# Attention and expert layer on one core: parts of queries and keys stored once, the repeats moved into the loads

## The chip, the cores and the metric

The kernel runs on one core of a Trainium2 chip. The metric is the device time of one execution in microseconds (us). Before the change three executions took 955.06, 957.02 and 960.02 us; the median is 957.02 us.

## The reference

The input is x with 8 batches of 512 tokens of 128 numbers, all in 32-bit floats. For each batch an attention block and then an expert block are computed:

```python
q = split_heads(einsum('bsd,kd->bsk', x, q_proj_weight))      # 16 heads of 8 numbers
k, v = the same with k_proj_weight, v_proj_weight
scores = einsum('bhtc,bhkc->bhtk', q, k) * 8 ** -0.5          # causal: -inf above the diagonal
out = einsum('bhtk,bhkc->bhtc', softmax(scores), v)           # heads side by side, then o_proj_weight
x = layernorm(x + out @ o_proj_weight.T)
# experts: 64 experts of width 64, sigmoid router, 4 of 8 groups, 8 experts kept, weights scaled by 2.5
h = silu(x @ Wg[e]) * (x @ Wu[e]) * coef[:, e]                # for every expert e; coef is 0 where not chosen
x = layernorm(x + sum_e h @ Wd[e] + silu(x @ SWg) * (x @ SWu) @ SWd)
```

All 64 experts are computed for all tokens, and the coefficient is zero where an expert is not chosen.

## The kernel before

**Parts.** A score is a product of 8 numbers for each head, and it is needed nearly in 32-bit precision, while the matmuls run on bf16. So each query and each key is split into three bf16 parts, whose sum is the number. The nine products of a part of q with a part of k are all taken in one matmul: its contraction has 3 x 3 x 8 = 72 rows. The stack of queries holds, in row (a, b, c), part a of the number c of the query; the stack of keys holds in that row part b. Each part thus stands three times in its stack.

**Way of the parts.** `q` and `k` (L776) project a batch; ScalarE writes part 0 (L900), VectorE the rest and parts 1 and 2 (L1148, L1154, L1157) into `qk_parts`, 128 rows (c, head) by 512 tokens. `store_part` stores one part to DRAM, in one DMA that writes it three times (L645): `q_rows_dram` and `k_rows_dram` have the dimensions [2 batches, a, b, c, head, token], part p of q goes to [a = p, all b], part p of k to [all a, b = p]. There are six stores a batch, counted by `parts_stored`. Then the task `rs` loads the rows of two heads, 72 rows of 2 x 512 bf16 numbers (2 KB a row), into both stacks (L700), two DMAs. Eight `rs` tasks a batch fill the stacks; these are rings of four places for a pair of heads (`RING_PAIRS` = 4), and `stacked[j]` counts the landings of place j, 16 for each DMA.

**Users of the stacks.** The task `mx` computes the scores of a head in three steps (L790), from which VectorE takes the largest of each row (L1182). When four heads are done, `mn` and `mT` turn the negated maxima into two further rows of the stack of queries (`max_rows`, L1207, loaded by L707), and the task `st` computes the transposed scores less the maximum from 96 rows (L808). ScalarE takes the exponential (L914), `pv` multiplies with v (L820). The `rs` for the place of an older pair waits until the last `st` of that pair is done.

**Experts.** For each of 32 pairs of experts and one shared unit TensorE computes gate (`g`) and up (`u`), three matmuls each (L749 to L751), and the down product (`d`, L864 to L866 or L879). GpSimd multiplies with the coefficients (L993), which a DMA has spread over the 128 rows (`coef_b`, L726, one for two units, 512 KB of writes each), and computes the low part for `d` (L997).

**Order.** There is no runtime planner. The tables FIRST, SECOND, THIRD, STEADY and EXPERTS give each task a place on a line, `order()` sorts them, and each engine goes through that one list and does its share of each task, in that order, with waits on semaphores. The attention of batch n + 1 is interleaved with the experts of batch n. Every DMA is issued by the sync engine's queue (SP), which is therefore in order too: a task whose wait is not over holds up everything behind it. Until the first expert TensorE does filler matmuls that nobody reads (L745, `FILL`; 62 after the first v).

Of the kernel before, what the change touches and what calls it, by code (L numbers as in the profile page):

```python
# [8 lines left out]
BF16 = mybir.dt.bfloat16  # L9
# [4 lines left out]
P = 128  # L14
B, S, D = 8, 512, 128
NH, C = 16, 8
# [15 lines left out]
STACK_PAIRS = NH // 2  # L32
RING_PAIRS = RING // 2
SPLIT_BY_DVE = 3
CHUNKS = 9
PARTS = 3
MAX_PARTS = 2
QK_ROWS = PARTS * PARTS * C
# [393 lines left out]
def build(nc, x, xT, wqT, wkT, wvT, woT, rwT, bias, Wg, Wu, Wd, SWgu, SWd, ident, causal, out):  # L432
    x_tok = x.rearrange("(b t p) d -> b p t d", t=NT, p=P)
    out_tok = out.rearrange("(b t p) d -> b p t d", t=NT, p=P)

    q_rows_dram = nc.dram_tensor("q_rows_dram", [2, PARTS, PARTS, C, NH, S], BF16).ap()
    k_rows_dram = nc.dram_tensor("k_rows_dram", [2, PARTS, PARTS, C, NH, S], BF16).ap()

    coef_dram = nc.dram_tensor("coef_dram", [2, E, S], F32).ap()

# [4 lines left out]
    with ExitStack() as ctx:  # L445
# [29 lines left out]
        qk_parts = sb("qk_parts", [P, 2, PARTS, S], BF16)  # L475
        rest = sb("rest", [P, S])
        q_stack = sb("q_stack", [STACK, RING, S], BF16)
        k_stack = sb("k_stack", [STACK, RING, S], BF16)
# [53 lines left out]
        stacked = [sem(f"stacked{j}") for j in range(RING_PAIRS)]  # L532
# [99 lines left out]
        def ring_nth(seg, n, j):  # L632

            return sum(t[0] == "rs" and t[2] % RING_PAIRS == j % RING_PAIRS and (t[1], t[2]) <= (n, j)
                       for t in seg.tasks)


        @block.sync
        def _(sp):
            sp.dma_start(wq_sb[:, :], wqT).then_inc(wq_in, 16)  # L640

            def store_part(kind, par, p):

                dst = q_rows_dram[par, p] if kind == "q" else k_rows_dram[par, :, p]
                sp.dma_start(dst.rearrange("o c h t -> (c h) o t"),  # L645
                             qk_parts[:, kind == "k", p, :].unsqueeze(1).to_broadcast([P, PARTS, S]))\
                    .then_inc(parts_stored, 16)

            def tasks(seg):
                for kind, n, i in seg.tasks:  # L650
                    task = (kind, n, i)
                    par = n % 2
                    if kind == "wld":
                        place = chunks[i][4]
                        if i - 2 >= SPLIT_BY_DVE:

                            sp.wait_ge(lo_done, i - 2 - SPLIT_BY_DVE + 1)
                        sp.dma_start(chunks[i][3], chunks[i][0]).then_inc(split_in[place], 16)
                    if kind == "ld":

                        after(sp, seg, sm_full, BANK_SM, ("v", n - 1, 0))
                        sp.dma_start(xT_sb[:, :], xT[n]).then_inc(x_in, 16)
                        if n == 0:
                            sp.dma_start(wk_sb[:, :], wkT).then_inc(wkv_in, 16)
                            sp.dma_start(wv_sb[:, :], wvT).then_inc(wkv_in, 16)
                    if kind == "ldtok":

                        before = seg.last(("x1",), task)
                        if before:
                            after(sp, seg, ob_free, BANK_O, ("oproj", before[1], 0))  # L670
                        after(sp, seg, out_ready, ("finx",), seg.last(("finx",), task))
                        sp.dma_start(y[:, :, :], x_tok[n]).then_inc(xtok_in, 16)
                    if kind == "q" and n == 0:
                        sp.dma_start(id_sb[:, :], ident).then_inc(id_in, 16)
                        sp.dma_start(hid[:, 1, :], causal).then_inc(id_in, 16)
                    if kind == "rs" and (n, i) == (0, 1):
                        for dst, src in small:
                            sp.dma_start(dst[:, :], src).then_inc(w_in, 16)
                    if kind in ("q", "k"):

                        for j in range(STACK_PAIRS - RING_PAIRS, STACK_PAIRS):
                            if seg.nth(("rs",), ("rs", n - 2, j)):
                                sp.wait_ge(stacked[j % RING_PAIRS], 16 * 2 * ring_nth(seg, n - 2, j))
                        after(sp, seg, part1_done, ("q", "k"), task)
                        store_part(kind, par, 0)
                    if kind in ("qsplit", "ksplit") and i == 1:
                        after(sp, seg, parts_done, ("q", "k"), (kind[0], n, 0))
                        for p in range(1, PARTS):
                            store_part(kind[0], par, p)
                    if kind == "rs" and (n, i) == (0, 0):  # L690
                        sp.wait_ge(zero_done, 2)
                        sp.wait_ge(const_done, 1)
                    if kind == "rs":

                        after(sp, seg, parts_stored, ("q", "k"), ("k", n, 0), 16 * PARTS)
                        before = (n, i - RING_PAIRS) if i >= RING_PAIRS else (n - 1, i + STACK_PAIRS - RING_PAIRS)
                        after(sp, seg, st_full, ("st",), ("st", before[0], 3 * 2 * (before[1] + 1) - 1))
                        hs, j = slice(2 * i, 2 * i + 2), i % RING_PAIRS
                        for stack, dram in ((q_stack, q_rows_dram), (k_stack, k_rows_dram)):
                            sp.dma_start(stack[0:QK_ROWS, 2 * j:2 * j + 2, :],  # L700
                                         dram[par, :, :, :, hs].rearrange("a b c h t -> (a b c) h t"))\
                                .then_inc(stacked[j], 16)
                    if kind == "mT":

                        after(sp, seg, sm_free, BANK_SM, (kind, n, i))
                        dst = q_stack[QK_ROWS:QK_ROWS + MAX_PARTS, HG * i % RING:HG * i % RING + HG, :]
                        sp.dma_start(dst.rearrange("p h (t q) -> p (h t) q", q=P), max_rows[:, :])\  # L707
                            .then_inc(maxrows_in[i], 16)
                    if kind == "attT" and n == B - 1:
                        after(sp, seg, ob_full, BANK_O, ("pv", n, GROUPS - 1))  # L710
                        sp.dma_start(wd_again, Wd[:, 0:PAIRS // 2 * D]).then_inc(wd_in, 16)
                    if kind == "coefT":
                        after(sp, seg, ob_free, BANK_O, task)
                        for t in range(2):
                            sp.dma_start(coef_dram[par].rearrange("e (k t q) -> t e k q", t=2, q=P)[t],
                                         coef_T[t * E:(t + 1) * E, :].rearrange("e (k q) -> e k q", q=P))\
                                .then_inc(coef_stored, 16)
                    if kind == "c":
                        after(sp, seg, coef_stored, ("coefT",), ("coefT", n, 0), 16 * 2)

                        before = ("h", n, 2 * i - 2) if i >= 2 else ("h", n - 1, UNITS - 3 + 2 * i)
                        after(sp, seg, h_done, ("h",), before)


                        src = coef_dram[par, 4 * i:4 * i + 4].rearrange("(e j) t -> e (j t)", e=2)
                        sp.dma_start(coef_b[:, i % 2, :, :].rearrange("p j t -> p (j t)"),  # L726
                                     src.unsqueeze(0).to_broadcast([I, 2, 2 * S])).then_inc(c_in[i % 2], 16)
                    if kind == "finx" and i == NT - 1:
                        after(sp, seg, out_ready, ("finx",), (kind, n, i))
                        sp.dma_start(out_tok[n], out_sb[:, :, :]).then_inc(out_stored, 16)  # L730

            tasks(ALL)
            sp.wait_ge(out_stored, 16 * B)


        @block.tensor
        def _(pe):
# [15 lines left out]
            def tasks(seg):  # L753
                before = None
                for kind, n, i in seg.tasks:
# [26 lines left out]
                    if kind == "mx":  # L782

                        h, part = divmod(i, 3)
                        if i % (3 * 2) == 0 and seg.nth(("rs",), ("rs", n, h // 2)):
                            pe.wait_ge(stacked[h // 2 % RING_PAIRS], 16 * 2 * ring_nth(seg, n, h // 2))
                        col = 0
                        for qb in MX_PARTS[part]:
                            wide = (qb + 1) * P
                            mm = pe.matmul(sm[:, col:col + wide], q_stack[0:QK_ROWS, h % RING, qb * P:(qb + 1) * P],  # L790
                                           k_stack[0:QK_ROWS, h % RING, 0:wide], start=True, stop=True)
                            col += wide
                        mm.then_inc(sm_full, 1)
# [511 lines left out]
```

## Time and profile before

| | |
|---|---|
| median of three executions | 957.02 us |
| span of the profiled execution (first to last instruction) | 952.6 us |
| mean granted clock of TensorE | 0.992 of 2.4 GHz |
| busy: TensorE, VectorE, GpSimd, ScalarE | 98%, 79%, 63%, 49% |
| moved by DMA | 121.70 MB |
| read from and written to HBM | 98.37 MB and 22.02 MB |

The profile is of one execution. PE is TensorE's matmuls and PEld its weight loads, DVE is VectorE, ACT ScalarE, POOL GpSimd, SPq the queue of the sync engine. The time of that execution differs from its span by what lies before the first and after the last instruction. A busy PE includes the fillers, and starts of matmuls overlap the end of the one before. From 340 us on one batch looks like the next (109 us each); the head (to about 125 us) and the end (from about 830 us) don't.

### The profile page before, as it was taken

How to read it: one execution, taken by the hardware profiler on the slowest of the kernel's cores; microseconds unless marked ns; L12 is line 12 of the kernel's file. 1: busy time of each engine (PE TensorE's matmuls, PEld its weight loads, DVE VectorE, ACT ScalarE, POOL GpSimd, SP SyncE). 2: the span in 40 equal slices, each digit the busy share in tenths (PEclk: the TensorE clock that was granted, in tenths of full speed). 3: DMA queues.
4: the chain of work that ended last, by engine and by line, in shares of the span. 5: the costliest groups of instructions: out<-in, count | busy, mean ns of one | idle time of the engine just before them, and what ended most of it. 6: DMA issues, size and time to landing. Idle time of an engine off the chain costs nothing.

```text
span 952.6 us, 16050 instructions
## 1 busy us (share of the span) xinstructions
PE 932.2 (98%) x5008; PEld 581.8 (61%) x5008; DVE 750.5 (79%) x2374; ACT 462.6 (49%) x866; POOL 598.4 (63%) x651
## 2 busy tenths in 40 slices
PE   8899999999999999999999999999999999999996
PEld 3355566666666666666666666675666666666664
DVE  5776887799877997799967997699967996578664
ACT  3355455455555545555555545555545555533221
POOL 2342247775777657775767757776667767775653
PEclk9799999999999999999999999999999999999998
DMA  8552154334534253433534254242633323242431
GB/s 292 159 167 67 50 176 146 113 104 136 181 96 135 92 184 126 136 114 96 192 115 136 84 179 138 94 136 73 211 117 113 114 88 95 87 162 82 138 129 56
DMA packets 64340, 121.70 MB, mean 128 GB/s; under 512 B 6656, under 2 KB 36224, under 8 KB 63744
## 3 DMA queue, kind: packets, MB, share of 16 engines
q1 hardware_dynamic: 64256, 120.67, 39.6%
q8 instruction: 41, 0.67, 0.3%
q14 instruction: 43, 0.35, 0.1%
HBM read 98.37 MB, written 22.02 MB: 126 GB/s over the span
## 4 chain that ended last, share of the span: by engine, by line
PE 85%; DVE 9%; issue 2%; DMA 2%; ACT 1%; SPq 0%; POOL 0%; POOLq 0%; DVEq 0%; ACTq 0%
PE acc L879 12%; PE ob L820 7%; PE sm L790 7%; PE st L808 7%; PE pu L749 6%; PE pg L749 5%; PE pg L751 5%; PE pg L750 5%; PE pu L750 5%; PE pu L751 5%; PE acc L745 4%; PE acc L864 2%; PE acc L866 2%; PE acc L865 2%; PE ob L832 2%
## 5 line engine op out<-in xcount | busy, mean ns | idle before, releaser
L993 POOL TENSOR_TENSOR hid<-hid,coef_b 128x512 f32<-128x512 f32 x240 | 309.5, 1290 | 134.7 <-DVE hid L1250 106.0
L1182 DVE CUSTOM_DVE_ANT_0 max_out<-sm,causal_sb 128x128 bf16<-128x128 f32 (+3 forms) x512 | 236.1, 486 | 60.6 <-PE sm L790 58.6
L942 ACT ACTIVATE hid<-pg 128x512 f32<-128x512 f32 x243 | 145.3, 598 | 245.2 <-PE pg L751 236.6
L914 ACT ACTIVATE probs<-st 128x512 f32<-128x512 f32 (+1 forms) x384 | 192.5, 525 | 75.8 <-PE st L808 74.1
L1241 DVE SCALAR_TENSOR_TENSOR hid<-hid,pg 128x512 f32<-128x512 f32 x243 | 165.8, 682 | 51.1 <-ACT hid L942 50.8
L997 POOL TENSOR_TENSOR hid_lo<-hid,hid_hi 128x512 fp32r<-128x512 f32 x112 | 144.0, 1285 | 75.7 <-ACT hid_hi L949 75.3
L1250 DVE TENSOR_TENSOR hid<-hid,pu 128x512 f32<-128x512 f32 x235 | 160.3, 682 | 30.0 <-PE pu L751 27.8
L979 POOL TENSOR_SCALAR_AFFINE_SELECT probs<-probs 128x256 f32<-128x256 f32 x256 | 97.8, 408 | 75.3 <-ACT probs L914 75.3
L790 PE MATMUL sm<-k_stack,q_stack 72*128 72x128 bf16 (+3 forms) x512 | 132.8, 307 | 3.7 <-DMA k_stack<-k_rows_dram 1.9
L749 PE MATMUL pg<-x_hi,wg_hi 128*128 128x512 f32 x240 | 127.7, 532 | 0.3 <-DVE hid L1241 0.2
L808 PE MATMUL st<-q_stack,k_stack 96*128 96x512 bf16 (+3 forms) x512 | 125.9, 304 | 0.2
L879 PE MATMUL acc<-hid,wd_sb 128*128 128x512 f32 x246 | 125.9, 593 | 0.0
L749 PE MATMUL pu<-x_hi,wu_hi 128*128 128x512 f32 x240 | 122.7, 511 | 0.9 <-DVE hid L1250 0.9
L751 PE MATMUL pg<-x_hi,wg_lo 128*128 128x512 f32 x240 | 94.8, 395 | 0.0
L750 PE MATMUL pu<-x_lo,wu_hi 128*128 128x512 f32 x240 | 94.8, 395 | 0.0
L751 PE MATMUL pu<-x_hi,wu_lo 128*128 128x512 f32 x240 | 94.7, 395 | 0.0
L750 PE MATMUL pg<-x_lo,wg_hi 128*128 128x512 f32 x240 | 94.6, 394 | 0.0
L808 PEld LDWEIGHTS st<-q_stack,k_stack 96*128 96x128 bf16 x512 | 45.1, 98 | 71.6 <-issue 52.9
L949 ACT ACTIVATE hid_hi<-hid 128x512 fp32r<-128x512 f32 x112 | 70.6, 630 | 36.5 <-POOL hid L993 31.6
L790 PEld LDWEIGHTS sm<-k_stack,q_stack 72*128 72x128 bf16 x512 | 43.7, 99 | 64.7 <-issue 41.4
L745 PE MATMUL acc<-filler 128*128 128x512 bf16 x240 | 81.0, 400 | 1.5 <-DVE filler L1019 1.5
L820 PE MATMUL ob<-probs,v_sb 128*32 128x512 f32 (+3 forms) x1024 | 75.6, 436 | 0.0
(161 smaller groups left out, 1295.4 us busy)
## 6 DMA issues: line engine op xcount, KB each, us to landing
coef_b<-coef_dram SPq DMA_DIRECT2D x128, 512.0 KB, 3.9
q_rows_dram<-qk_parts SPq DMA_DIRECT2D x24, 384.0 KB, 4.1
k_rows_dram<-qk_parts SPq DMA_DIRECT2D x24, 384.0 KB, 3.5
q_stack<-q_rows_dram SPq DMA_DIRECT2D x64, 144.0 KB
k_stack<-k_rows_dram SPq DMA_DIRECT2D x64, 144.0 KB
xT_sb<-in_xT SPq DMA_DIRECT2D x8, 256.0 KB, 3.8
y<-in_x SPq DMA_DIRECT2D x8, 256.0 KB, 3.9
out<-out_sb SPq DMA_DIRECT2D x8, 256.0 KB, 2.6
```

The costliest lines, as they stand in the source:

```text
L749: pe.matmul(psum[:, :], hi, x1_hi[:, par, :], start=True, stop=False)
L750: pe.matmul(psum[:, :], hi, x1_lo[:, par, :], start=False, stop=False)
L751: return pe.matmul(psum[:, :], lo, x1_hi[:, par, :], start=False, stop=True)
L790: mm = pe.matmul(sm[:, col:col + wide], q_stack[0:QK_ROWS, h % RING, qb * P:(qb + 1) * P], k_stack[0:QK_ROWS, h % RING, 0:wide], start=Tru ...
L808: mm = pe.matmul(st_bank[i % 2][:, col:col + wide], k_stack[:, h % RING, kb * P:(kb + 1) * P], q_stack[:, h % RING, kb * P:S], start=True, ...
L879: pe.matmul(acc[:, :], w, hid_of(n, i), start=first, stop=last).then_inc(d_full, 1)
L914: act.activation(probs[:, h % HG, at:at + wide], st_bank[i % 2][:, 0:wide], ACT.Exp, scale=C ** -0.5).then_inc(exp_done, 1)
L942: act.activation(hid_of(n, i), gate_bank(n, i)[:, :], ACT.Tanh, scale=0.5).then_inc(tanh_done, 1)
L993: pool.tensor_tensor(hid_of(n, i), hid_of(n, i), coef_b[:, half % 2, j, :], ALU.mult)\
L1182: last = dve.tensor_tensor_reduce(out=max_out[:, seg.nth(BANK_SM, task) % 2, col:col + wide], in0=sm_of(seg, task)[:, col:col + wide], in1 ...
L1241: dve.scalar_tensor_tensor(hid_of(n, i), hid_of(n, i), 1.0, gate_bank(n, i)[:, :], ALU.add, ALU.mult).then_inc(a_done, 1)
L1250: ins = dve.tensor_tensor(hid_of(n, i), hid_of(n, i), up_bank(n, i)[:, :], ALU.mult)
```

## The change

`store_part` writes each part once, and the DRAM tensors lose a dimension. The loads into the stacks read each row three times: the one load of the stack of keys does it with a repeat of step zero in front of its source pattern, and the load of the stack of queries becomes three, one for each part a, each with such a repeat over b. The counts of `stacked` become 4 DMAs for a pair of heads. Everything else, the order too, is as before.

```diff
+STACK_LOADS = 4
-    q_rows_dram = nc.dram_tensor("q_rows_dram", [2, PARTS, PARTS, C, NH, S], BF16).ap()
-    k_rows_dram = nc.dram_tensor("k_rows_dram", [2, PARTS, PARTS, C, NH, S], BF16).ap()
+    q_rows_dram = nc.dram_tensor("q_rows_dram", [2, PARTS, C, NH, S], BF16).ap()
+    k_rows_dram = nc.dram_tensor("k_rows_dram", [2, PARTS, C, NH, S], BF16).ap()
...
-                dst = q_rows_dram[par, p] if kind == "q" else k_rows_dram[par, :, p]
-                sp.dma_start(dst.rearrange("o c h t -> (c h) o t"),
-                             qk_parts[:, kind == "k", p, :].unsqueeze(1).to_broadcast([P, PARTS, S]))\
+                dst = q_rows_dram[par, p] if kind == "q" else k_rows_dram[par, p]
+                sp.dma_start(dst.rearrange("c h t -> (c h) t"), qk_parts[:, kind == "k", p, :])\
                     .then_inc(parts_stored, 16)
...
-                                sp.wait_ge(stacked[j % RING_PAIRS], 16 * 2 * ring_nth(seg, n - 2, j))
+                                sp.wait_ge(stacked[j % RING_PAIRS], 16 * STACK_LOADS * ring_nth(seg, n - 2, j))
...
-                        for stack, dram in ((q_stack, q_rows_dram), (k_stack, k_rows_dram)):
-                            sp.dma_start(stack[0:QK_ROWS, 2 * j:2 * j + 2, :],
-                                         dram[par, :, :, :, hs].rearrange("a b c h t -> (a b c) h t"))\
-                                .then_inc(stacked[j], 16)
+                        for a in range(PARTS):
+                            rows = slice(a * PARTS * C, (a + 1) * PARTS * C)
+                            sp.dma_start(q_stack[rows, 2 * j:2 * j + 2, :].rearrange("r h t -> r (h t)"),
+                                         q_rows_dram[par, a, :, hs].rearrange("c h t -> c (h t)").unsqueeze(0)
+                                         .to_broadcast([PARTS, C, 2 * S])).then_inc(stacked[j], 16)
+                        sp.dma_start(k_stack[0:QK_ROWS, 2 * j:2 * j + 2, :].rearrange("r h t -> r (h t)"),
+                                     k_rows_dram[par, :, :, hs].rearrange("b c h t -> (b c) (h t)").unsqueeze(0)
+                                     .to_broadcast([PARTS, PARTS * C, 2 * S])).then_inc(stacked[j], 16)
...
-                            pe.wait_ge(stacked[h // 2 % RING_PAIRS], 16 * 2 * ring_nth(seg, n, h // 2))
+                            pe.wait_ge(stacked[h // 2 % RING_PAIRS], 16 * STACK_LOADS * ring_nth(seg, n, h // 2))
```

## Rows read from the trace of the kernel before

**Rows 1.** The page, busy time, share of the span and instructions of TensorE.
```profile
PE 932.2 (98%) x5008; PEld 581.8 (61%) x5008; DVE 750.5 (79%) x2374; ACT 462.6 (49%) x866; POOL 598.4 (63%) x651
```
**Rows 2.** The page, groups: busy us, mean ns; idle before and its releaser.
```profile
L790 PE MATMUL sm<-k_stack,q_stack 72*128 72x128 bf16 (+3 forms) x512 | 132.8, 307 | 3.7 <-DMA k_stack<-k_rows_dram 1.9
...
L745 PE MATMUL acc<-filler 128*128 128x512 bf16 x240 | 81.0, 400 | 1.5 <-DVE filler L1019 1.5
```
**Rows 3.** Stretches of the head: busy us by engine, clock, DMA share, GB/s.
```profile
10.00:12.00 2.00, 2.00 (x11) 0.90 (x10) 1.96 (x7) 0.40 (x1) 0.00 (x0) 1.00 1.02 338
22.00:24.00 2.00, 1.09 (x6) 0.38 (x5) 2.00 (x4) 0.49 (x1) 1.43 (x1) 1.00 0.97 358
24.00:26.00 2.00, 1.38 (x7) 0.40 (x7) 2.00 (x11) 0.00 (x0) 2.00 (x1) 1.00 0.99 344
26.00:28.00 2.00, 0.82 (x3) 0.11 (x2) 1.33 (x6) 0.00 (x0) 0.07 (x1) 1.00 1.04 303
30.00:32.00 2.00, 2.00 (x8) 0.57 (x5) 1.56 (x9) 0.66 (x1) 1.26 (x1) 0.50 0.71 250
```
**Rows 4.** The chain of waits in the head: start us, us, what.
```profile
11.83 4.72 DMA k_rows_dram<-qk_parts
...
20.28 7.67 DMA k_stack<-k_rows_dram
```
**Rows 5.** The page, DMA issues: count, KB each, median us to landing.
```profile
q_rows_dram<-qk_parts SPq DMA_DIRECT2D x24, 384.0 KB, 4.1
...
q_stack<-q_rows_dram SPq DMA_DIRECT2D x64, 144.0 KB
```
**Rows 6.** Stretches with one load's traffic: pair (438 to 440), coef_b (508), max_rows (506.4).
```profile
438.00:438.50 0.50, 0.50 (x4) 0.28 (x2) 0.50 (x6) 0.40 (x1) 0.50 (x3) 1.00 0.37 33
438.50:439.00 0.50, 0.50 (x6) 0.27 (x4) 0.50 (x2) 0.20 (x1) 0.25 (x1) 1.00 0.68 221
439.00:439.50 0.50, 0.50 (x4) 0.39 (x3) 0.47 (x3) 0.47 (x1) 0.00 (x0) 1.00 0.73 279
439.50:440.00 0.50, 0.50 (x4) 0.23 (x3) 0.50 (x2) 0.40 (x2) 0.00 (x0) 1.00 0.17 57
508.00:508.50 0.50, 0.50 (x4) 0.22 (x2) 0.39 (x1) 0.00 (x0) 0.50 (x1) 1.00 0.97 360
506.42:506.66 0.24, 0.24 (x12) 0.13 (x4) 0.00 (x0) 0.00 (x0) 0.24 (x1) 1.00 0.15 34
```
**Rows 7.** SP's queue, the issues of a pair: start us, us, line, out<-in.
```profile
437.21 0.30 SPq L700 DMA_DIRECT2D q_stack<-q_rows_dram  x1
437.56 0.36 SPq L700 DMA_DIRECT2D k_stack<-k_rows_dram  x1
```
**Rows 8.** SP's queue, first issues of pairs with little or no slack.
```profile
41.62 0.32 SPq L700 DMA_DIRECT2D q_stack<-q_rows_dram  x1
...
97.17 0.30 SPq L700 DMA_DIRECT2D q_stack<-q_rows_dram  x1
...
361.79 0.52 SPq L700 DMA_DIRECT2D q_stack<-q_rows_dram  x1
```
**Rows 9.** TensorE, the first matmuls that read these pairs.
```profile
44.90 0.21 PE L790 MATMUL sm<-k_stack,q_stack 72*128 72x128 bf16 x1
...
100.44 0.33 PE L790 MATMUL sm<-k_stack,q_stack 72*128 72x128 bf16 x2
...
366.43 0.33 PE L790 MATMUL sm<-k_stack,q_stack 72*128 72x128 bf16 x2
```
**Rows 10.** SP's queue, a max_rows load behind a pair, and a lone one.
```profile
478.33 0.29 SPq L700 DMA_DIRECT2D q_stack<-q_rows_dram  x1
...
479.08 0.72 SPq L707 DMA_DIRECT2D q_stack<-max_rows  x1
...
505.09 0.70 SPq L707 DMA_DIRECT2D q_stack<-max_rows  x1
```
**Rows 11.** TensorE, the first matmul that reads the maxima loaded at 479.08.
```profile
482.83 0.39 PE L808 MATMUL st<-q_stack,k_stack 96*128 96x512 bf16 x1
```

## The prediction, written before the changed kernel was run

> **What bounds the kernel now.** I read the engine shares first. TensorE's matmuls fill 98% of the span [rows 1], so time can only be won where TensorE stands still, and any new stand-still is paid in full unless it falls into one that is there already. Next come its groups [rows 2]: the score matmuls of L790, the readers of the two stacks, waited 3.7 us in all, 1.9 us of that for a stack load. TensorE's order is fixed, and a filler matmul (L745) keeps it busy through much of the head, so "busy" there does not mean "ahead".
>
> The stretches of the head [rows 3] show 1.09, 1.38 and 0.82 us of busy TensorE per 2 us between 22 and 28 us, the DMA engines full all the while (0.97 to 1.04), and then a clock of 0.50, the 1.2 GHz level. The chain of waits [rows 4] says who is late: the last store of key parts lands after 4.72 us, and the second k_stack load after 7.67 us. From 40 us on TensorE is the bound. The end of the kernel (from 830 us) has no stores of parts and no stack loads, and stays as it is.
>
> The profiled run has a span of 952.6 us, the median of the timed runs is 957.02, so 4.4 us lie around the span or between runs. I work on the span and add the difference to the median.
>
> **The stores.** 48 stores of 384 KB (24 of queries, as many of keys) become 48 of 128 KB [rows 5]: 12.6 MB less of 121.7. On the issuing queue a store cost about 0.4 us and still does. In the steady part nobody waits for them. In the head, six of them (1.57 MB less) stand ahead of everything in full engines: at 338 GB/s (10 to 12 us, [rows 3]) that is 4.6 us of DMA time. Without any other change TensorE could take from it its two waits at 22.2 and 26.8 us, 1.9 us, and, if the clock then stayed up, at most half of the 10.2 us at 0.50, 5.1 us. Bounds: 0 and 7.0 us of gain; a value of 3.5 would be fair if the loads stayed as they are.
>
> **The loads' issues.** Each pair of heads now costs four DMA issues, not two, 64 times. One takes 0.30 to 0.37 us with 0.05 between [rows 7]; the k_stack issue therefore starts 0.7 us later, and what is queued behind it (max_rows, coef_b, the next input) as well. SyncE's queue is mostly waiting, so this costs nothing where a transfer has slack, and 0.7 us where it has none.
>
> **The loads' spread over the DMA engines** is what decides. The trace has three shapes of it [rows 6]. A coef_b load, whose outermost count is 64 in the source and 128 in the tile, fills 0.97 of the engines. The stack loads of before, 72 rows on both sides, reach 0.68 and 0.73 and no more: 12 of 16 would be 0.75. A max_rows load, outermost count 2 in the stack and 32 in its source, fills 0.15: 2 of 16 would be 0.125. So the number of engines follows the outermost count of both sides: 12 is the largest number up to 16 that divides 72, 2 the largest that divides 2 and 32. The new loads have an outermost source count of 3 (the zero-step repeat comes first), with 24 or 72 rows in the stack. That gives 3 engines. A max_rows load uses 2 engines although it has 32 pieces, which speaks against the hope that pieces are dealt out whatever the shape.
>
> Price of one pair of loads. Before, 144 pieces of 2 KB on 12 engines, 12 each. In [rows 7] and [rows 6] the first issue is at 437.21, traffic runs from 438.1 to just under 440.0 and ends there: 2.8 us after the first issue; four pairs in the head are picked up by TensorE 3.26, 3.27, 3.28 and 3.72 us after their first issue [rows 8, 9], so notice of landing comes about 0.5 us after the last piece. Now 144 pieces on 3 engines are 48 each. The rate: 279 GB/s at a share of 0.73 [rows 6] is 24 GB/s for one engine, so 2 KB take 0.085 us and 48 take 4.1 us. From first issue to notice: 0.9 + 4.1 + 0.5 = 5.5 us against 3.3, that is 2.2 us later; the extra issues lie inside this, since they run while the three engines work. Bounds: 0 (twelve engines) and 3.1 us (nothing overlaps: 4.1 against 1.0); I take 2.2.
>
> The Trainium skill (DMA: Bandwidth & Descriptors, section "Why a DMA increments its semaphore by 16 and not by 1") says the number of engines is the largest up to 16 that divides the slowest dimension of both patterns, and its closing table warns of just this, a leading zero-stride broadcast of c copies. By that rule the sum is the one below; without it, it would be the 957 us of rival 1. The trace agrees in the three shapes above, but none of them has a zero step of fewer than 16 outermost.
>
> **Where the 2.2 us fall.** I compare, pair by pair, first issue and first use of the slot [rows 8, 9]. Issue-to-use of 3.3 us means no slack.
> - None: 41.62 to 44.90, 57.21 to 60.93, 69.64 to 72.90, 97.17 to 100.44 (the first and the last of the four are shown). 4 x 2.2 = 8.8 us.
> - Little: 82.66 to 86.36 and 116.17 to 120.13 (0.4 and 0.7 us): 1.8 + 1.5 = 3.3 us.
> - Later batches: most pairs have 4 to 11 us and lose nothing. The first pair of a batch is issued beside a coef_b load, which brings each engine eight pieces of 4 KB, 0.17 us each at the rate above, 1.1 to 1.4 us; so it needs some 6.6 us, and has 4.64 (361.79 to 366.43), 5.27 (470.27 to 475.54) and twice 5.6 us (the first is shown). One more pair (213.35 to 218.96) is like these. 1.9 + 1.3 + 1.0 + 1.0 + 1.0 = 6.2 us.
> These uses lie apart, and every load is issued after the stall before it is over, so one stall does not pay for the next. Sum 18.3 us.
>
> **What is queued behind.** A max_rows load uses two engines, by the same reasoning two of those three. A lone one, issued at 505.09 [rows 10], has its traffic done at 506.66 [rows 6]. At 479.08 one is issued 0.75 us after the first load of a pair, and TensorE reads what it brings at 482.83 [rows 10, 11]. The pair's pieces would now hold the three engines from 478.33 + 0.9 for 4.1 us, to 483.3; with 0.25 for its own and 0.5 for the notice it is there at 484.1: a stall of 1.3 us. There are four such places, alike in the last batches (uses at 373.7, 482.8, 592.0, 701.1 us), and four more (90.9, 156.2, 321.2, 755.4) where the pair was issued longer before, or the use comes later, for which I put 0.5 each: 5.2 + 2.0 = 7.2 us. The coef_b loads right behind a pair land 1 to 2 us later; GpSimd waits for them, its results are up to 0.8 us early for TensorE, and the max_rows stall just before covers most. I put 0.
>
> **The head up to 40 us.** The stores free 4.6 us on each engine, but each pair puts 3.1 us more on three of them (36 pieces of 0.085). Pair one is issued some 2.5 us earlier and lands before the fillers end: 0.6 us won. Pair two: 4.6 us less and 6.2 us more in front, so 1.6 us later than 27.95 [rows 4]. Net 1 us of loss at the first softmax step. Bounds: 3 won, 4 lost.
>
> **Sum:** 18.3 + 7.2 + 1.0 = 26.5 us. 952.6 + 26.5 = 979.1 for the span, 957.0 + 26.5 = 983.5 us predicted. On the size: stalls may be part absorbed (half: 970), or the loads queue worse beside coef_b (up to 1000).
>
> **Rivals.**
> 1. Twelve engines as before (the repeat is folded into rows). Then the stores win 3.5 us in the head, and the later k_stack issue costs 0.7 us at the four places without slack and 0.3 at another: 3.1 us. 957.0 - 3.5 + 3.1 = 956.6: not slower. It is decided by one thing, the share of the DMA engines during a pair: 0.7, not 0.2. For it: the total bytes of the loads are the same. Against: the max_rows shape. If the clock also stays up from 29 to 40 us, 7.0 - 3.1 = 3.9 us faster, 953.1; a little more than that would count as faster.
> 2. Three engines, and the stalls bring the clock down. Before, 2.6 us of stand-still within 22 to 28 us went before 10.2 us at 0.50. Six stalls of 1.5 to 2.2 us follow in the head; if four of them each bring such a stretch, at up to 5.1 us, 983.5 + 20.4 = 1004. Against: between them TensorE is denser than at 22 to 28 us.
> 3. Three engines, hidden: if the work behind the stalls had its own slack, only the four places without slack and the head would count, at half their price: 957.0 + 4.4 + 1.0 = 962.4. For it: the filler matmuls between them can be passed quickly. Against: TensorE takes its instructions in order, and after 40 us its own work is the bound.
>
> **Chances.** Forecast 0.67, rival 1 0.15 (0.03 of it under 952), rival 2 0.10, rival 3 0.06, and 0.02 for something else that is faster. A measurement of this kernel tells about 0.5% (4.8 us) from no change. Faster 0.03 + 0.02 = 0.05; same is the rest of rival 1 and part of rival 3, 0.12 + 0.02 = 0.14; slower 0.81. The range from 956 to 1006 takes in half of rival 1 and of rival 2, and all of rival 3; it leaves out 0.07 + 0.02 + 0.05 = 0.14.
>
> **What would show it.** Right: during a lone pair of loads in the steady part the DMA share is near 0.19, for some 4 us; TensorE waits for q_stack or k_stack loads about ten times, 1 to 2.5 us each, six of them before 125 us; the waits for max_rows loads grow; HBM writes fall from 22.0 to about 9.4 MB; the second k_stack load is still about 27 to 31 us. Wrong: a share near 0.7 in these loads, or waits for them of under 3 us in all. If the waits come out as said and the time does not follow, the stalls were absorbed; if the clock row shows new stretches at 0.50, it is rival 2.

## The result, and the profile after

The changed kernel takes 1081.65 us (median of four executions, 1070.77 to 1089.21), the kernel before beside it 956.71 us: a ratio of 1.1267, 95% interval 1.1205 to 1.133. It is 12.7% slower. I had said 2.8% (983.5 us, with 1006 as the upper end). The direction was right, and so was the confinement of the loads to three DMA engines; the loss was 4.7 times what I had said (125 us in place of 26.5), because two steps of the working were wrong, which the section on the prediction names. The execution that was profiled was the slowest of the four, 1089.21 us, and the ratio is that of the other three (1070.77 to 1083.41 us), so the sums below are some 10 us high.

The page first: span, busy engines, the row of clocks, and the two groups of score matmuls, which answer to [rows 1, 2]. "..." stands for lines left out.

```profile
span 1087.4 us, 16166 instructions
PE 980.3 (90%) x4996; PEld 604.7 (56%) x5008; DVE 753.2 (69%) x2374; ACT 464.6 (43%) x866; POOL 597.9 (55%) x651
...
PEclk9688998999998999999989989899998989999999
...
HBM read 98.37 MB, written 9.44 MB: 99 GB/s over the span
...
L794 PE MATMUL sm<-k_stack,q_stack 72*128 72x128 bf16 (+3 forms) x512 | 139.5, 321 | 43.1 <-DMA k_stack<-k_rows_dram 41.4
L812 PE MATMUL st<-q_stack,k_stack 96*128 96x512 bf16 (+3 forms) x512 | 131.8, 317 | 46.7 <-DMA q_stack<-max_rows 46.1
```

Of the kernel before, the row of clocks and the second group:

```profile
PEclk9799999999999999999999999999999999999998
...
L808 PE MATMUL st<-q_stack,k_stack 96*128 96x512 bf16 (+3 forms) x512 | 125.9, 304 | 0.2
```

TensorE's busy time grew by 48.1 us (932.2 to 980.3) though its work is the same (12 of 5008 records are missing in this trace), and its idle time by 86.7 us; together they are the 134.8 us that the span grew (952.6 to 1087.4). Nearly all of the new idle time stands in front of two groups: L794 waited 3.7 us before and 43.1 now, L812 0.2 us before and 46.7 now. All other idle time together grew by 0.8 us. The 48 us of "busy" go with the clock: its 8s and lower digits stand all along the row, where before only the head and the last microseconds had any. In the clock record the stretches at 0.50 sum to 121.1 us, 17.4 before; if work at half speed takes twice as long, the 103.7 us more would give 52 (an estimate).

By place: the first batch's output projection starts at 128.4 us where it was 94.7, so a quarter of the loss (33.7 us) has come by then; from the fourth batch to the seventh a batch takes 126.5 us where it took 109, which makes 70 us. The stores did what they were to do: 9.44 MB written, 22.02 before.

**One pair of loads.** The next rows are SP's queue at a pair that no other load disturbs (start us, us), and the DMA share (the column before the last) in four of the microseconds behind it. They answer to [rows 6, 7].

```profile
393.18 2.24 SPq L701 DMA_DIRECT2D q_stack<-q_rows_dram  x3
395.46 0.69 SPq L704 DMA_DIRECT2D k_stack<-k_rows_dram  x1
```

```profile
395.00:396.00 1.00, 1.00 (x6) 0.54 (x6) 1.00 (x4) 0.74 (x3) 0.94 (x4) 1.00 0.09 33
396.00:397.00 1.00, 1.00 (x6) 0.73 (x4) 1.00 (x5) 0.58 (x2) 1.00 (x1) 1.00 0.20 76
...
398.00:399.00 1.00, 1.00 (x5) 0.55 (x3) 1.00 (x5) 0.00 (x0) 1.00 (x1) 1.00 0.19 74
...
400.00:401.00 1.00, 1.00 (x9) 0.69 (x7) 1.00 (x2) 0.39 (x1) 1.00 (x3) 1.00 0.00 0
```

The share never passes 0.20, and 3 of 16 is 0.19: three engines. But the four issues take 2.97 us, 0.69 each, where I had 0.30 to 0.37. The traffic starts 1.5 us after the first issue (0.9 before) and is over at +6.4 us; the notice of landing comes at +6.75 us. Four other such pairs landed after 6.60 to 6.79 us, and one, at 130.91, after 7.71. Before, lone pairs were there after 3.0 to 3.3 us. A pair costs 3.6 us more, not 2.2. The traffic itself takes 4.9 us, not 4.1: the share of 0.09 early on shows the three engines half idle while the next load is still being issued. And most pairs are not alone: over all 64 the median landing went from 3.30 to 7.65 us, so beside coef_b and max_rows loads a pair costs more like 4.3 us.

**One place where both waits fall.** SP's queue and TensorE's readers near 430 us, in the first of the batches that look alike; they answer to [rows 9 to 11].

```profile
436.71 2.15 SPq L701 DMA_DIRECT2D q_stack<-q_rows_dram  x3
438.90 0.69 SPq L704 DMA_DIRECT2D k_stack<-k_rows_dram  x1
439.63 0.69 SPq L711 DMA_DIRECT2D q_stack<-max_rows  x1
```

```profile
433.94 0.33 PE L794 MATMUL sm<-k_stack,q_stack 72*128 72x128 bf16 x2 [3.21 <-DMA k_stack<-k_rows_dram]
...
445.18 0.39 PE L812 MATMUL st<-q_stack,k_stack 96*128 96x512 bf16 x1 [3.79 <-DMA q_stack<-max_rows]
```

The maxima of four heads were ready when SP was still issuing the pair. So their load is issued 2.9 us after the first of the pair where it was 0.75, and then meets the pair's pieces (this pair, with a coef_b load issued behind it, landed only after 8.2 us): 5.50 us from its issue to landing, 2.4 us before. The median over the 32 max_rows loads went from 2.36 to 4.33 us, and 20 of them now make TensorE wait.

### The profile page after: what moved, and what is told of

It reads as the page before. It is cut to its first block, busy times and chain, and to the rows that moved or that the text cites. A ratio compares the mean times of both kernels' runs of the same rounds, so it can differ in the third digit from the quotient of the medians.

```text
span 1087.4 us, 16166 instructions
## 1 busy us (share of the span) xinstructions
PE 980.3 (90%) x4996; PEld 604.7 (56%) x5008; DVE 753.2 (69%) x2374; ACT 464.6 (43%) x866; POOL 597.9 (55%) x651
## 3 DMA queue, kind: packets, MB, share of 16 engines
HBM read 98.37 MB, written 9.44 MB: 99 GB/s over the span
## 4 chain that ended last, share of the span: by engine, by line
PE 60%; DMA 18%; SPq 9%; DVE 8%; issue 3%; POOL 2%; ACT 1%; POOLq 0%; DVEq 0%
PE acc L883 10%; DMA q_stack<-max_rows 9%; DMA k_stack<-k_rows_dram 7%; SPq L701 6%; PE st L812 5%; PE sm L794 5%; PE pu L753 4%; PE pg L753 4%; PE pg L755 4%; PE pg L754 4%; PE pu L754 4%; PE pu L755 4%; PE ob L836 2%; PE acc L749 2%; PE ob L824 2%
## 5 line engine op out<-in xcount | busy, mean ns | idle before, releaser
L794 PE MATMUL sm<-k_stack,q_stack 72*128 72x128 bf16 (+3 forms) x512 | 139.5, 321 | 43.1 <-DMA k_stack<-k_rows_dram 41.4
L812 PE MATMUL st<-q_stack,k_stack 96*128 96x512 bf16 (+3 forms) x512 | 131.8, 317 | 46.7 <-DMA q_stack<-max_rows 46.1
L883 PE MATMUL acc<-hid,wd_sb 128*128 128x512 f32 x246 | 134.9, 631 | 0.0
L753 PE MATMUL pg<-x_hi,wg_hi 128*128 128x512 f32 x240 | 131.9, 550 | 0.3 <-DVE hid L1245 0.2
L753 PE MATMUL pu<-x_hi,wu_hi 128*128 128x512 f32 x240 | 127.3, 531 | 0.9 <-DVE hid L1254 0.9
L812 PEld LDWEIGHTS st<-q_stack,k_stack 96*128 96x128 bf16 x512 | 46.7, 102 | 125.8 <-DMA q_stack<-max_rows 53.9
L794 PEld LDWEIGHTS sm<-k_stack,q_stack 72*128 72x128 bf16 x512 | 45.1, 102 | 109.0 <-issue 88.3
L754 PE MATMUL pu<-x_lo,wu_hi 128*128 128x512 f32 x240 | 98.0, 408 | 0.0
L755 PE MATMUL pu<-x_hi,wu_lo 128*128 128x512 f32 x240 | 97.6, 407 | 0.0
L755 PE MATMUL pg<-x_hi,wg_lo 128*128 128x512 f32 x240 | 97.4, 406 | 0.0
L754 PE MATMUL pg<-x_lo,wg_hi 128*128 128x512 f32 x240 | 96.9, 404 | 0.0
```

Source lines behind the costliest of these rows:

```text
L753: pe.matmul(psum[:, :], hi, x1_hi[:, par, :], start=True, stop=False)
L754: pe.matmul(psum[:, :], hi, x1_lo[:, par, :], start=False, stop=False)
L755: return pe.matmul(psum[:, :], lo, x1_hi[:, par, :], start=False, stop=True)
L812: mm = pe.matmul(st_bank[i % 2][:, col:col + wide], k_stack[:, h % RING, kb * P:(kb + 1) * P], q_stack[:, h % RING, kb * P:S], start=True, ...
L883: pe.matmul(acc[:, :], w, hid_of(n, i), start=first, stop=last).then_inc(d_full, 1)
```

## The experiments

All times below are medians, with the ratio to the kernel before on the same chip. "A", "B", "C" are the theories that the expectations name: A is the small number of engines with a dear issue, B the repeated reading, C the number of issues; D and E are about the clock. A lone pair is one beside which no other load runs. The diffs are shortened.

**Repeat inside, wide outside (e1).** Still four loads and parts stored once, but the rows of the stacks are ordered (a, c, b), so that no pattern begins with 3 (q_stack's load begins with 24, k_stack's three with 8).

```diff
-  three q_stack loads, source [3 (step 0), 8, 1024]; one k_stack load, source [3 (step 0), 24, 1024]
+  sp.dma_start(q_stack[...72 rows...], q_rows_dram[par, :, :, hs].rearrange("a c h t -> (a c) (h t)")
+               .unsqueeze(1).to_broadcast([PARTS * C, PARTS, 2 * S]))
+  for a in range(PARTS):
+      sp.dma_start(k_stack[...24 rows of a...], k_rows_dram[par, :, :, hs].rearrange("b c h t -> c b (h t)"))
```

> The changed kernel with the stack rows ordered (a, c, b), still four DMAs a pair and the parts still stored once: one load of q_stack repeats each of 24 source rows (outermost count 24), three loads of k_stack read 8 x 3 rows (outermost 8). Theory A (the outermost count of 3 confines a load to 3 DMA engines and makes its issue dear, 0.69 us): the engines become 12 and 8, the waits of TensorE for stacks and max_rows fall from 87 us to under 15, the clock stays up, time 955 to 975 us. Rival B (reading a DRAM row three times is what is slow): the q_stack loads still repeat, time over 1040. Rival C (four DMA issues a pair instead of two are what is slow): still four, over 1040.

Measured: 973.38 us, ratio 1.0172 (1.0131 to 1.0212). Theory A. 108 of the 125 us are gone, with the same number of loads and the same bytes. Every row is still read three times, those of queries inside one load and those of keys by three loads. The issue is as dear as it was: SP's queue and the two groups of TensorE in this kernel.

```profile
342.54 0.82 SPq L699 DMA_DIRECT2D q_stack<-q_rows_dram  x1
343.41 2.09 SPq L704 DMA_DIRECT2D k_stack<-k_rows_dram  x3
```

```profile
L794 PE MATMUL sm<-k_stack,q_stack 72*128 72x128 bf16 (+3 forms) x512 | 131.8, 305 | 8.7 <-DMA k_stack<-k_rows_dram 5.8
...
L812 PE MATMUL st<-q_stack,k_stack 96*128 96x512 bf16 (+3 forms) x512 | 125.8, 304 | 8.3 <-DMA q_stack<-max_rows 7.3
```

The four issues still take 2.96 us, but with 8 and 12 engines a lone pair lands after 4.4 to 4.8 us and TensorE waits 17.0 us in these groups, not 89.8.

**Four plain loads (e3).** The kernel before, with its q_stack load cut into three of 24 rows.

```diff
-  sp.dma_start(q_stack[0:QK_ROWS, ...], q_rows_dram[par, :, :, :, hs].rearrange("a b c h t -> (a b c) h t"))
+  for a in range(PARTS):
+      sp.dma_start(q_stack[rows, ...], q_rows_dram[par, a, :, :, hs].rearrange("b c h t -> (b c) h t"))
```

> The kernel before, each part stored three times, but q_stack loaded by three DMAs of 24 rows (outermost 24): four DMAs a pair, 12 engines, no repetition. Theory A: an issue stays near 0.3 us, the k_stack load starts 0.7 us later, 957 to 963 us. Rival C (the number of issues): most of the 125 us, over 1040. Rival B: 957.

Measured: 960.39 us, ratio 1.0040 (1.0016 to 1.0063). With plain patterns on 12 engines, two loads more a pair cost 3 to 4 us. An issue of a plain pattern takes 0.36 us, and the four of a pair 1.53 us; the median pair lands 0.46 us later than before.

**Two that missed their aim (e4, e5).** Here the source was only written as 3 x 24 (and 3 x 8) rows, in memory one even row of rows. I expected three engines.

> The kernel before, two DMAs a pair, each part stored three times, no row read twice; only the source pattern of the two loads is written as 3 x 24 rows instead of 72. Theory A: 3 engines, 48 pieces of 2 KB each one after the other, 4.1 us, issue about 0.7 us each: pair lands 6.1 to 6.5 us after its first issue, against 3.3 before and 6.7 in the changed kernel; 1045 to 1080 us. Rivals B and C: 957.

> The kernel before with each part stored three times and no row read twice, but with the four loads and the outermost counts (3) of the changed kernel. It differs from the changed kernel by the stores and the repetition alone. Theory A: 1075 to 1095 us, a few us above the changed kernel, since the first stores are three times as long. Rival B: 957 to 965. Rival C: 1080.

Measured: 956.57 us (ratio 0.9997, 0.9979 to 1.0016) and 962.20 us (1.0059, 1.0040 to 1.0079). Both are misses for theory A as I had put it. The trace says why: the load instructions carry a destination of [72,1] rows, as before, where those of e9 below carry [1,72], and issue in 0.30 us (e4), as before. So the two levels had been merged when the program was built. They repeat the kernel before and e3, and they tell that the pattern counts as it is in the instruction, after merging, not as it is written.

**Three engines without any repetition (e9, e10).** One unused place of padding in the DRAM tensors keeps the levels apart. Parts are stored three times, and no row is read twice.

```diff
-  q_rows_dram = nc.dram_tensor("q_rows_dram", [2, PARTS, PARTS, C, NH, S], BF16).ap()
+  q_rows_dram = nc.dram_tensor("q_rows_dram", [2, PARTS, PARTS + 1, C, NH, S], BF16).ap()[:, :, 0:PARTS]
   (k_rows_dram alike; in e10 q_rows_dram has C + 1 in place of PARTS + 1, and four loads)
+  dram[par, :, :, :, hs].rearrange("a b c h t -> a (b c) (h t)")      # e9: 3 x 24 rows, two loads a pair
```

> The kernel before (parts stored three times, two loads a pair, no row read twice), with one place of padding in the DRAM tensors, so that the 3 x 24 source rows no longer merge into 72. Theory A (an outermost count of 3 means 3 engines, and a pattern with two levels an issue of 0.7 us): 48 pieces an engine, the pair lands 1.5 + 4.1 + 0.5 = 6.1 us after its first issue, 1035 to 1075 us. Rival B (reading a DRAM row three times is slow): 957 us. Rival C (four issues instead of two): 957 us.

> The changed kernel's four loads with outermost counts of 3, but parts stored three times in padded tensors and no row read twice. It differs from the changed kernel by stores and repetition alone. Theory A: 1075 to 1095 us, the issues 0.7 us each, a pair's issues over 2.9 us. Rival B: 957 to 970. Rival C: 1080.

Measured: e9 1066.56 us, ratio 1.1141 (1.111 to 1.1171); e10 1097.58 us, ratio 1.1481 (1.146 to 1.1501), 2.6 us above my range. That settles it: with the number of loads of before, two a pair, and each byte from its own place, a pattern that begins with 3 makes the kernel some 110 us slower. It changes two things at once, the three engines and the form with two levels; e14 below has two levels on nine engines and loses 15 us, so the step from nine engines to three is some 95. Rivals B and C both said 957. SP's queue and the DMA share in e9:

```profile
391.27 0.74 SPq L700 DMA_DIRECT2D q_stack<-q_rows_dram  x1
392.05 0.71 SPq L700 DMA_DIRECT2D k_stack<-k_rows_dram  x1
```

```profile
394.00:395.00 1.00, 1.00 (x6) 0.78 (x5) 1.00 (x5) 0.68 (x2) 1.00 (x1) 1.00 0.19 76
```

A lone pair lands after 6.35 to 6.9 us in e9 and after 7.0 to 7.6 in e10, and the traffic of one takes 4.6 and 5.4 us. So with three engines and two levels, two loads more a pair cost 31 us (e9 to e10), eight times what they cost in e3: theory C is out as the cause of the 125 us, but the number of loads is not free once each is dear and narrow. e10 is 16 us slower than the changed kernel by the medians (20 by the ratios); it differs by its stores, three times as long, and by rows that are not repeated. Both may count: the first `st` starts at 44.6 us in e10 and at 40.9 in the changed kernel, and a lone pair, beside which no store runs, lands some 0.5 us later in e10 (7.22 at 406.8 against 6.75 at 393.2). So repetition was no burden here. What each of the two is worth was not tested.

**Half of the load confined (e8).** One q_stack load on 12 engines, one k_stack load with the repeat outermost, 24 pieces on each of three engines.

```diff
+  q_stack <- q_rows_dram[par, :, :, hs].rearrange("a c h t -> (a c) (h t)").unsqueeze(1).to_broadcast([24, 3, 2 * S])
+  k_stack <- k_rows_dram[par, :, :, hs].rearrange("c b h t -> (c b) (h t)").unsqueeze(0).to_broadcast([3, 24, 2 * S])
```

> The changed kernel with two loads a pair: q_stack by one load with outermost count 24 (12 engines, each row read three times), k_stack by one load with the repeat outermost (3 engines, 24 pieces each, 2.0 us). Parts stored once (those of keys with outermost count 8). Theory A: k_stack lands 0.8 + 1.0 + 2.0 + 0.5 = 4.3 to 4.9 us after the pair's first issue, between before (3.3) and changed (6.7): 970 to 1000 us. Rival B: near the changed kernel, 1060 to 1085, for all bytes are still read three times. Rival C (the count of issues): 957.

Measured: 1007.34 us, ratio 1.0529 (1.0497 to 1.0562). It lies between, as A says, 7 us above my range; a lone pair lands after 5.2 to 5.8 us, where I had 4.3 to 4.9.

**Nine engines (e14).** Padding that leaves 9 x 8 rows: is the issue dear because few engines are used, or because the pattern has two levels?

> The kernel before (stores three times, two loads a pair, no row read twice), with padding that leaves 9 x 8 source rows unmerged: outermost count 9, so 9 engines, and a pattern of two levels. Theory A in two parts: the issue of a two-level pattern costs 0.7 us whatever the number of engines, and 9 engines have 16 pieces each, 1.4 us. The pair lands about 0.6 + 0.4 + 0.4 = 1.4 us later than before (4.4 to 4.7 us after its first issue), 960 to 970 us. If the dear issue came from having few engines, the issues stay near 0.35 us and the time is 957 to 960.

Measured: 970.78 us, ratio 1.0156 (1.0135 to 1.0177).

```profile
342.47 0.81 SPq L700 DMA_DIRECT2D q_stack<-q_rows_dram  x1
343.32 0.77 SPq L700 DMA_DIRECT2D k_stack<-k_rows_dram  x1
```

It is the pattern of these loads and not the number of engines: 0.8 us on nine engines, 0.7 on three, 0.3 to 0.36 for one level. Their traffic starts 1.5 us after the issue with two levels and 0.9 us with one. Two levels do not always cost that much: a coef_b load, 64 x 2 rows of 4 KB on 16 engines, is issued in 0.52 us and starts its traffic after 1.3. A lone pair lands after 4.1 to 4.4 us, 1.1 to 1.3 us later than before, by the second level and by nine engines in place of 12; together they are worth 15 us. The time lies 0.8 us above my range, the landing at or below the 4.4 to 4.7 that I had.

The semaphore events of the traces fit the engine counts. A stack load raised its semaphore in 13 events in the kernel before, in 4 in the changed kernel and in e9, in 10 in e14, in 13 (queries) and 9 (keys) in e1, a max_rows load in 3: each time one more than the engines that I count.

So the 125 us can be walked step by step, each step with its measured kernel: two levels and nine engines, +15 (e14); nine to three, +95 (e9); two loads a pair to four, +31 (e10); rows repeated and small stores, -16 (the changed kernel). The steps are worth this in this order; in another order they may differ, as e3 shows for the third.

**Stores alone (e13).** One store of 128 rows in place of the threefold one; loads in the old shape.

```diff
-  sp.dma_start(dst.rearrange("o c h t -> (c h) o t"), qk_parts[...].unsqueeze(1).to_broadcast([P, PARTS, S]))
+  sp.dma_start(flat[kind == "k"][par].rearrange("(p r t) -> p r t", p=PARTS, t=S)[p], qk_parts[:, kind == "k", p, :])
```

> The kernel before with the stores alone changed: each part is stored once. The loads keep their shape (two a pair, 72 rows of 2 KB, 12 engines, no repetition) but bring other rows of that tensor, so the scores are not those of the reference; the work is the same. It measures what the saved 12.6 MB are worth. From the prediction: 3.5 us faster, bounds 0 and 7: 950 to 957 us. If DMA time in the head were the bound of the whole head: 950. If nobody waits for it: 956 to 958.

Measured: 954.32 us, ratio 0.9984 (0.9973 to 0.9995). The change is worth 0.16%, about 1.5 us, and not all of it need be the 12.6 MB: the loads bring other rows here, and lone pairs land 0.1 to 0.3 us earlier (mostly 2.8 to 3.0 us). The saved DMA time was not what the head waited for: TensorE still stands 2.68 us before the second pair (25.58 to 28.26), which was used at 28.09 before. What differs in the head is the stretch at 0.50, which lasts 3.4 us (from 28.9) where it was 10.2; that this is what won the time is not shown.

**Filled stalls (e6).** The changed kernel, with fillers in the gaps, to separate the clock from the waits. The same is done ahead of the waits for maxima, there behind the wait for the bank.

```diff
+  for _ in range(STALLS.get(task, 0)):                     # 35 places, 2 to 17 each, 326 in all
+      pe.matmul(sm[:, :], filler[:, 0:P], filler[:, :], start=True, stop=True)
   pe.wait_ge(stacked[h // 2 % RING_PAIRS], 16 * STACK_LOADS * ring_nth(seg, n, h // 2))
```

> The changed kernel with 326 filler matmuls more on TensorE, ahead of the waits for stacks and maxima at the 35 places where the changed kernel stood still for over 0.7 us, sized to 0.85 of each gap (they write a bank that the next real matmul overwrites). Theory D (of the loss of some 130 us about 50 is the clock at 1.2 GHz, brought down by the stalls): the stretches at 0.50 fall from 121 us to under 50, and the time from 1082 to 1030 to 1055 us. Rival E (the half-speed stretches cost nothing of their own, since TensorE would have waited anyway): 1075 to 1095 us.

Measured: 1062.42 us, ratio 1.1106 (1.1079 to 1.1134). Between D and E, in the range of neither. The page's row of clocks:

```profile
PEclk9899999999999999999999999999999999999999
```

The stretches at 0.50 fall from 121.1 to 26.3 us, but the time only by 15 us by the ratios and 19 by the medians, where D said 27 to 52. The trace says where. The output projection of the first batch starts at 128.5 us with the fillers and at 128.4 without: in the head the fillers gained nothing, most likely since TensorE would have waited for the same loads. From the fourth batch to the seventh it is 121 us a batch against 126.5, and 109 before. So some 5 us of the 17.5 a batch are clock, and 12.5 are waits. Both figures are rough: the two profiled executions lie 24.5 us apart, more than the kernels do, which makes 5 a high figure, while some fillers may have cost a little themselves, which makes it a low one.

**A version for use (e11).** Keys stored three times and loaded plainly, first; queries stored once, one load on 12 engines.

> A version for use: rows in the order (a, c, b). Parts of keys are stored three times (three stores each, outermost count 8) and loaded by one plain load of 72 rows, issued first; parts of queries are stored once and loaded by one load with outermost count 24 that repeats each row (12 engines, issue 0.8 us). Theory A: the pair lands 0.4 us later than before, the head gains 0 to 2 us from the shorter stores of queries, but has nine stores of keys: 955 to 962 us. Faster than before only if the stores of queries are on the head's path.

Measured: 977.62 us, ratio 1.0241 (1.0218 to 1.0265). A miss: 15 us above my range. A lone pair lands after 3.5 to 3.9 us, about 0.5 later than before, as expected. But the group that waits is now

```profile
L795 PE MATMUL sm<-k_stack,q_stack 72*128 72x128 bf16 (+3 forms) x512 | 134.1, 310 | 13.0 <-DMA q_stack<-q_rows_dram 11.0
```

and 10.1 of the 11.0 us lie before 125 us (2.70 us from 22.8, 1.85 from 30.0, 2.99 from 64.6 and so on), so the head ends later. How much of that is the nine stores of keys and how much the query load was not tested. No kernel of this study that computes the reference is faster than the kernel before by more than the noise.

## Why the prediction was wrong

- **Three engines.** Right, and the decision hung on it: the share is at most 0.20 in a lone pair. That it is what costs is shown by e9 with e14 (no repetition in either, three engines 1066.6 us, nine 970.8) and its reverse, e1 (repetition without three engines, 973.4 us). Rival 1, the twelve engines, is out.
- **"One takes 0.30 to 0.37 us"** and **"the extra issues lie inside this"** are the first step that failed. I took the issue's price from plain patterns. A stack load with two levels costs 0.7 to 0.8 us and starts its traffic 0.6 us later. Of before, the max_rows load had shown 0.72 us in [rows 10], and I read over it. And a q_stack load of 24 pieces keeps three engines busy for 8 x 0.084 = 0.67 us, less than the 0.77 us from one issue to the next, so the engines wait for the issues. In place of 0.9 + 4.1 + 0.5 = 5.5 us, a lone pair took 1.53 + 4.89 + 0.33 = 6.75. Price of a pair: 3.6 us, not 2.2, and 4.3 by the median of all pairs.
- **"These uses lie apart" and "most pairs have 4 to 11 us and lose nothing".** Places held, sizes did not. In the head I had six stalls of 1.5 to 2.2 us; there were seven beyond the first three pairs' (2.3, 3.0, 3.5, 4.4, 2.9, 4.4, 3.4 us), each about the price of a pair and more. After 170 us there were six, of 0.8 to 3.2 us, 12.1 us in all where I had 6.2. All waits before L794: 39.4 us more, where my sum had 18.3 plus the head's 1.0. The first `st` started 3.7 us later (40.90 against 37.17), inside the bounds of that 1.0 but far from it.
- **"5.2 + 2.0 = 7.2 us" for what is queued behind** is the worst mis-sized term: 46.5 us. I had moved the max_rows load by the pair's traffic alone. With the pair's issues at 2.9 us it is itself issued 2.2 us later, and that holds at many more places: 20 loads in place of my eight, up to 3.8 us each. The zero that I put on coef_b held for TensorE's waits (0.8 us for all other groups).
- **The clock** I had as rival 2 at 0.10, with four stretches in the head and 20 us. It came nearly everywhere, 104 us more at 0.50; filling the stalls gained 15 to 19 us (e6), and that in the steady batches and not in the head. The sum had no term for it.
- **The stores:** "a value of 3.5 would be fair" for what they give; e13 measured 1.5, not all of it surely the stores'.
- **The range** ended just above rival 2's 1004 and treated the two main sums as separate, though they had one common factor, the price of a pair. If that is 60% too low, all stalls with slack grow by more than 60%, since the slack is taken off first. The max_rows load of [rows 10] landed at 481.53 and was read at 482.83, 1.3 us of slack: the delay that I had, 2.6 us, costs 1.3. The load at 439.63 landed 8.4 us after its pair's first issue where it had been 3.2: 5.2 us of delay, which would cost 3.9, and TensorE waited 3.79.

## What to carry to other kernels

Read a DMA's outermost count on both sides, as it stands after merging, before moving a repeat into it: a zero step of 3 in front took these loads from 12 engines to 3, and with two levels their issue took twice as long. Put the repeat inside and a wide dimension outside: the loads with 24 and 8 outermost (e1) cost 17 us where the changed kernel's cost 125, but they cost something still. And where a queue is in order, price what waits behind a dearer step by its issue time as well as by its traffic, and count the places by their slack, which was small in this tuned order.

## What the runs showed of the hardware that I had not expected

- Issue of a load on SP's queue: 0.30 to 0.36 us for one level of rows (72 or 24), 0.66 to 0.82 us for a stack load of two levels, on 3, 8, 9 and 12 engines alike; first traffic 0.9 us and 1.5 us after its start. A coef_b load of two levels on 16 engines: 0.52 us, and 1.3 us to the first traffic.
- Landing of a pair of 288 KB after its first issue, undisturbed: 3.0 to 3.3 us on 12 engines plain, 4.1 to 4.4 on nine, 4.4 to 4.8 on 12 and 8 (four loads), on three 6.35 to 6.9 (e9, two loads), 6.6 to 6.8 (changed kernel, four loads, one pair 7.7) and 7.0 to 7.6 (e10, four loads without repeats).
- Reading each DRAM row three times was no slower than reading three copies (changed kernel 1081.7 us, e10 1097.6, which also has the longer stores; a lone pair 6.75 against 7.22 us).
- In the steady part of the changed kernel (from 340 us) 15 stalls of 1.8 to 3.8 us between dense work brought TensorE to 1.2 GHz for 3.4 or 6.8 us at a time, and three of 1.6 to 3.2 us (at 433.9, 729.8 and 761.1) did not. With the stalls filled (e6) two such stretches were left there.
